# A decoder stack on one core: stream attention outputs normalised with head rows on the partitions, closing products in column tiles

## The chip, the cores and the metric

The kernel runs on one core of one Trainium2 chip. The metric is the device time of one execution in microseconds; the time of a kernel is the median over its runs.

## The reference, cut to what matters

Two decoder layers on a sequence of 2048 rows of 256 features, with a context of 1601 rows. What the change touches is the self-attention and the cross-attention of the second layer (16 heads of 16 features each), whose outputs are projected, added to the input and normalised:

```python
qkv = (jnp.einsum('bnd,ed->bne', x, qkv_w) + qkv_b).reshape(b, n, H, 3 * HD)
q, k, v = ...
attn = jax.nn.softmax(jnp.einsum('bhqd,bhkd->bhqk', q, k) * SCALE, axis=-1)
out = jnp.einsum('bhqk,bhkd->bhqd', attn, v)
...
x = _layernorm(x + _L1_attn_ref(x, ...))         # out @ fc_w.T + fc_b + x
x = _layernorm(x + _L1_xattn_ref(ctx_1024, ctx_1024, x, ...))   # out @ Wo + bo
```

Before it run the first layer (banded attention with a GELU network, causal cross-attention, a network with eight low-rank experts), behind it the eight-expert network of the second layer.

## The kernel before

The second layer's two attentions run as one stream, `decoder_attention`. `Plan` writes its order out by hand. A **step** is one segment (0 self-attention, 1 cross-attention), one chunk of 512 queries (`QC`, four per segment) and one group of four heads (`GH`): 2 x 4 x 4 = 32 steps. A **pair** is a step and one tile of 128 keys: 16 pairs in a step of segment 0, 13 in one of segment 1, 464 in all. `plan.first[s]` is the first pair of step s. Every engine walks over the pairs p = 0 ... 495 in order, and at each p does what the plan lists there.

In a pair TensorE (PE) does the scores of four heads (L1481, bf16, four column tiles of 32 columns side by side), the products with the values of the pair before (L1499, f32, again 32 columns per head, so that the four heads fill `ps_o`), and, between them, the products for the row maxima of the **next** step (L1291), which go through a ring of three PSUM banks `ps_m` (`plan.bank`, `bank_free`). ScalarE (ACT) takes the exponentials (L1612). VectorE (DVE) reduces each maxima product (L1304): 64 of them in a step of segment 0, 64 in one of segment 1, of which 16 have 128 columns only. The same ring carries all small products of the stream.

SyncE (SP) issues the transfers in program order. At p = first[s+1] it issues `load(s+3)`, held until the scores up to that pair are done: 12 transfers, six of keys (L1269) and six of queries (L1272), to rows taken six apart.

The end of a step s: ACT copies `ps_o` to `o_raw` (`copy_o`, L1605) at p = first[s+1]. Its row 32j + 16 holds the sum of the exponentials of head j, rows 32j to 32j + 15 the unnormalised output. Two pairs later (`TURN_AT`) PE transposes it in four full-array f32 transposes to a ring bank (`turn_out`, L1509), and DVE takes the reciprocal of 16 columns (L1726) and multiplies into `o_tok` (L1728), both in `normalise`. After four steps a chunk is complete, and at the four pairs that follow PE transposes each token tile back (`turn_tokens`, L1519, two transposes), ACT copies it to `o_fm` (L1622), and a pair later PE does the output product (`out_product`, L1532, two full-array f32 products of 256 columns), which DVE adds to `x_tok` (L1739) and follows with the statistics. Root, scaling and a transpose back (L1542) come later. The projections of segment 1's keys, queries and values are woven in as units (L1558, 16 of them) and value tiles (L1567, 13 of them), full-array f32 products too.

Of the kernel before, what the change touches and what calls it, by code (L numbers as in the profile page):

```python
# [1107 lines left out]
class Plan:  # L1108
# [11 lines left out]
    TURN_AT = 2  # L1120

    def __init__(self, segments):
        self.segments = segments
        self.steps = [(si, c, g) for si in range(len(segments)) for c in range(NQ) for g in range(NG)]
        self.pairs, self.first = [], []
        for s, (si, c, g) in enumerate(self.steps):
            self.first.append(len(self.pairs))
            self.pairs += [(s, i, kt) for i, kt in enumerate(segments[si].at.key_tiles(c))]
        self.total = len(self.pairs)
        self.first.append(self.total)  # L1130
        self.chunks = [(si, c) for si in range(len(segments)) for c in range(NQ)]
        self.out_at = [self.first[s + 1] + (self.TURN_AT if s + 1 < len(self.steps) else 1)
                       for s in range(len(self.steps))]
# [42 lines left out]
    def close_chunks(self, project_next):  # L1176


        for k, (si, c) in enumerate(self.chunks):
            start = self.out_at[NG * k + NG - 1]  # L1180
            for a in range(QT):
                self.tasks[start + 1 + a].append(("turn", k, a))
                self.tasks[start + 2 + a].append(("prod", k, a))
            self.tasks[start + 7].append(("root", k))
            self.tasks[start + 8].append(("inverse", k))
            for a in range(QT):
                self.tasks[start + 8 + a].append(("scale", k, a))
                self.tasks[start + 9 + a].append(("fm", k, a))
            if project_next and si == 0:
                for m in range(DT):  # L1190
                    self.unit(start + 15 + 2 * m, "q", m, c * QC, QC)
                for a in range(QT):
                    self.tasks[start + 20 + a].append(("base", k, a))
# [18 lines left out]
    def set_ring(self, banks):  # L1212

        self.banks, self.order = banks, []
        for p in range(self.total + 32):
            if p < self.total:
                self.order += [("max", x) for place in self.places[p] for x in place]
            self.order += [("out", s) for s in range(len(self.steps)) if self.out_at[s] == p]
            self.order += [task for task in self.tasks[p] if task[0] in ("turn", "prod", "fm", "unit", "v")]
        self.index = {step: r for r, step in enumerate(self.order)}  # L1220
# [115 lines left out]
def decoder_attention(nc, name, plan, maxima, q_st, x_tok, x_fm, ctx_fm, t, cst):  # L1336
# [17 lines left out]
    with ExitStack() as ctx:  # L1354
# [3 lines left out]
        def sem(n):  # L1358
# [3 lines left out]
        inv_den = sb("inv_den", [P, QT, GH, 1], F32)  # L1362
        o_raw = sb("o_raw", [P, QC], F32)
        prob = sb("prob", [P, 2, GH, QC], F32)
        o_tok = sb("o_tok", [P, 2, QT, D], F32)
        o_fm = sb("o_fm", [P, 2, DT, P], F32)
# [16 lines left out]
        s_scores, s_prob, s_pv, s_msc, s_mred, s_ocopy, s_turn, s_inv_den, s_norm = map(  # L1383
            sem, ("scores", "prob", "pv", "msc", "mred", "ocopy", "turn", "inv_den", "norm"))
        s_oturn, s_ofm, s_prod, s_base, s_y, s_stat, s_mv, s_std, s_inv, s_x, s_xturn, s_xfm = map(
            sem, ("oturn", "ofm", "prod", "base", "y", "stat", "mv", "std", "inv", "x", "xturn", "xfm"))
# [8 lines left out]
        def step_of(p):  # L1395
            return plan.pairs[p][0]

        @block.sync
        def _(sp):
# [20 lines left out]

            sp.dma_start(ctx_sb[:, :, 0:CTX], ctx_fm.rearrange("(t p) n -> p t n", p=P)).then_inc(s_ctx, 16)
# [9 lines left out]
            for p in range(plan.total + 32):  # L1431
# [14 lines left out]
        def _(pe):  # L1446
            def bank_free(step):
# [7 lines left out]
                elif kind == "out":  # L1455
                    pe.wait_ge(s_norm, user[1] + 1)
                elif kind == "turn":
                    pe.wait_ge(s_ofm, user[1] * QT + user[2] + 1)
# [44 lines left out]
            def turn_out(s):  # L1503

                step = ("out", s)
                pe.wait_ge(s_ocopy, s + 1)
                bank_free(step)
                for a in range(QT):
                    mm = pe.transpose(plan.bank(step)[:, a * P:(a + 1) * P], o_raw[:, a * P:(a + 1) * P],  # L1509
                                      cst["ident"][:, :])  # L1510
                mm.then_inc(s_turn, 1)

            def turn_tokens(step):

                k, a = step[1:]
                pe.wait_ge(s_norm, NG * (k + 1))
                bank_free(step)
                for m in range(DT):
                    mm = pe.transpose(plan.bank(step)[:, m * P:(m + 1) * P], o_tok[:, k % 2, a, m * P:(m + 1) * P],  # L1519
                                      cst["ident"][:, :])  # L1520
                mm.then_inc(s_oturn, 1)

            def out_product(step):
# [22 lines left out]
            def unit_product(step):  # L1546
# [10 lines left out]
                for d in range(DT):  # L1557
                    mm = pe.matmul(plan.bank(step)[:, 0:n], w_sb[:, 0 if side == "q" else 1, d, m * P:(m + 1) * P],  # L1558
                                   src[:, d, k:k + n], start=(d == 0), stop=(d == DT - 1))
                mm.then_inc(s_mm, 1)  # L1560

            def v_product(step):
# [3 lines left out]
                for d in range(DT):  # L1566
                    mm = pe.matmul(plan.bank(step)[:, 0:D], ctx_sb[:, d, i * P:(i + 1) * P], w_sb[:, 2, d, :],  # L1567
                                   start=(d == 0), stop=(d == DT - 1))
                mm.then_inc(s_vmm, 1)

            for p in range(plan.total + 32):
# [11 lines left out]
                for s in range(len(plan.steps)):  # L1583
                    if plan.out_at[s] == p:
                        turn_out(s)
                for task in plan.tasks[p]:
                    if task[0] == "turn":
                        turn_tokens(task)
                    elif task[0] == "prod":
# [9 lines left out]
        def _(act):  # L1599
            def copy_o(s):  # L1600

                act.wait_ge(s_pv, plan.first[s + 1])
                if s > 0:
                    act.wait_ge(s_turn, s)
# [9 lines left out]

            def copy_tokens(step):

                k, a = step[1:]
                n = k * QT + a
                act.wait_ge(s_oturn, n + 1)
                if n >= 2:  # L1620
                    act.wait_ge(s_prod, n - 1)
                act.activation(o_fm[:, n % 2, :, :], plan.bank(step)[:, 0:D].rearrange("p (a b) -> p a b", a=DT),  # L1622
                               ACT.Copy).then_inc(s_ofm, 1)
# [30 lines left out]
            for p in range(plan.total + 32):  # L1654
# [5 lines left out]
                for task in plan.tasks[p]:  # L1660
                    if task[0] == "turn":
                        copy_tokens(task)
                    elif task[0] == "root":
# [42 lines left out]
        def _(dve):  # L1706
# [9 lines left out]
            def normalise(s):  # L1716

                si, c, g = plan.steps[s]
                k = s // NG
                heads = plan.bank(("out", s))[:, :].rearrange("p (a j d) -> p a j d", a=QT, j=GH)  # L1720
                dve.wait_ge(s_turn, s + 1)
                if s > 0:
                    dve.wait_ge(s_norm, s)
                if g == 0 and k >= 2:
                    dve.wait_ge(s_oturn, QT * (k - 1))
                dve.reciprocal(inv_den[:, :, :, :], heads[:, :, :, SH:SH + 1]).then_inc(s_inv_den, 1)  # L1726
                dve.wait_ge(s_inv_den, s + 1)
                dve.tensor_tensor(o_tok[:, k % 2, :, g * GH * SH:(g + 1) * GH * SH]  # L1728
                                  .rearrange("p a (j d) -> p a j d", d=SH), heads[:, :, :, 0:SH],
                                  inv_den[:, :, :, :].to_broadcast((P, QT, GH, SH)), ALU.mult).then_inc(s_norm, 1)  # L1730
# [49 lines left out]
            for p in range(plan.total + 32):  # L1780
# [3 lines left out]
                for s in range(len(plan.steps)):  # L1784
                    if plan.out_at[s] == p:
                        normalise(s)
# [754 lines left out]
def decoder_kernel(nc, t, out):  # L2541

    nc.disable_value_cache = True
    with ExitStack() as ctx:
# [9 lines left out]
        y_slots = nc.dram_tensor("y_slots", (EXPERT_TILES * P, D), F32).ap()  # L2554
        s_zero = nc.alloc_semaphore("slots_cleared")
# [59 lines left out]
        with ExitStack() as c:  # L2615
# [11 lines left out]
            decoder_attention(nc, "d1", plan, maxima, q_st, x_tok, x_fm, t["ctx_fm"], t, cst)  # L2627
# [87 lines left out]
```

## Time and profile before

| | |
|---|---|
| median of 3 runs (lowest to highest) | 3201.78 us (3201.13 to 3211.98) |
| profiled execution, its own time | 3196.11 us |
| its span | 3194.4 us |
| mean granted TensorE clock | 0.938 of full speed |
| busy, whole span | PE 2806.6 us (88%), DVE 2064.1 (65%), ACT 1568.5 (49%), POOL 224.4 (7%) |
| the stream: first scores, last copy of `ps_o` | 1321.9 us, 2718.8 us |

The busy shares are of the whole program; the stream is some 1400 us of it. Of the windows in the first group below, one is a plain step of segment 0, the other a plain step of segment 1. Times below are from the span's start. A matmul's record overlaps the next one's, so the price of a group on PE is read from the start of one group to the start of the next, and not from its length. PE groups of x4 are four column tiles side by side.

### The profile page before, as it was taken

The page shows a single profiled execution, that of the slowest core. Times are in us where ns is not written, and L with a number is a line of the kernel's source. Part 1 is how long each engine was busy: PE and PEld are TensorE (multiplying, and loading weights), DVE is VectorE, ACT ScalarE, POOL GpSimd, SP SyncE. Part 2 cuts the span into 40 slices and gives each one's busy share as a digit, 9 for nine tenths or more (in the row PEclk, how much of TensorE's full clock was granted, in tenths as well). Part 3 has the DMA queues.
Part 4 walks back from the last instruction along what each step waited for, and adds up shares of the span by engine and source line. Part 5 has one row for each costly group of instructions (what it writes and reads, how often), then busy time and mean ns, then how long its engine had stood idle before and what let it go on. Part 6 is the DMA issues. An engine that isn't in the chain of part 4 may idle for free. (4 is left out here: it accounts for less than half of the span.)

```text
span 3194.4 us, 83729 instructions
## 1 busy us (share of the span) xinstructions
PE 2806.6 (88%) x34974; PEld 1416.8 (44%) x34975; DVE 2064.1 (65%) x4240; ACT 1568.5 (49%) x2122; POOL 224.4 (7%) x295
## 2 busy tenths in 40 slices
PE   6677987999996997799999999999999999369993
PEld 3465552444534564134434343443433333246662
DVE  4335136888855235688999898988998995312224
ACT  2223222666672322266767776776666768123331
POOL 2001201000001002300000000000000000210003
PEclk9888997999997999699999999999999999589997
DMA  5322023011001003312112112111111110611102
GB/s 155 102 60 67 27 72 100 13 39 39 3 2 37 1 0 109 99 42 67 34 53 51 53 36 60 44 44 51 42 49 44 44 44 2 249 49 33 33 31 89
DMA packets 112871, 173.46 MB, mean 54 GB/s; under 512 B 17882, under 2 KB 88427, under 8 KB 112147
## 3 DMA queue, kind: packets, MB, share of 16 engines
q1 hardware_dynamic: 109460, 160.11, 17.5%
q0 software_dynamic: 3072, 8.39, 0.8%
q8 instruction: 266, 4.36, 0.6%
q14 instruction: 73, 0.60, 0.1%
HBM read 127.63 MB, written 40.51 MB: 53 GB/s over the span
## 5 line engine op out<-in xcount | busy, mean ns | idle before, releaser
L1304 DVE TENSOR_REDUCE d_part_max<-d_ps_m 128x1 f32<-128x512 f32 (+1 forms) x1964 | 1128.1, 631 | 89.0 <-PE d_ps_m L1291 52.7
L1612 ACT ACTIVATE d_prob<-d_ps_s 128x1024 f32<-128x1024 f32 x928 | 898.7, 1022 | 345.7 <-PE d_ps_s L1481 338.9
L1291 PE MATMUL d_ps_m<-k_st,q_st 97*32 97x512 bf16 (+1 forms) x5296 | 479.2, 361 | 20.5 <-DVE d_part_max L1304 16.9
L1481 PE MATMUL d_ps_s<-q_st,k_st 98*32 98x512 bf16 x5104 | 439.5, 382 | 9.7 <-ACT d_prob L1612 8.4
L690 DVE TENSOR_REDUCE x_part_max<-x_att_ps_m 128x1 f32<-128x512 f32 (+2 forms) x578 | 309.6, 587 | 50.2 <-PE x_att_ps_m L675 22.7
L936 ACT ACTIVATE x_att_prob<-x_att_ps_s 128x1024 f32<-128x1024 f32 (+3 forms) x296 | 258.8, 920 | 138.8 <-PE x_att_ps_s L817 82.8
L1499 PE MATMUL d_ps_o<-d_prob,a_values 128*32 128x512 f32 x2048 | 265.0, 592 | 0.0
L1291 PEld LDWEIGHTS d_ps_m<-k_st,q_st 97*32 97x32 bf16 x5296 | 141.5, 95 | 274.2 <-DVE d_part_max L1304 127.8
L1291 PE MATMUL d_ps_m<-q_st 97*32 97x512 bf16 (+1 forms) x2560 | 230.9, 361 | 2.2 <-DVE d_part_max L1304 0.4
L1481 PEld LDWEIGHTS d_ps_s<-q_st,k_st 98*32 98x32 bf16 x5104 | 136.6, 97 | 196.0 <-issue 82.4
L1499 PE MATMUL d_ps_o<-d_prob,x_values 128*32 128x512 f32 x1664 | 215.5, 593 | 0.4 <-ACT d_prob L1612 0.4
L666 PE MATMUL x_att_ps_m<-k_st,q_st 97*32 97x512 bf16 (+3 forms) x2312 | 202.8, 343 | 3.3 <-DVE x_part_max L690 2.7
L1481 PE MATMUL d_ps_s<-q_st 98*32 98x512 bf16 x2320 | 200.2, 380 | 2.6 <-ACT d_prob L1612 2.6
L817 PE MATMUL x_att_ps_s<-q_st,k_st 98*32 98x512 bf16 (+3 forms) x2368 | 192.3, 358 | 11.0 <-DMA q_st<-x_neg_row 6.5
L2465 ACT ACTIVATE l1f_h_cols<-l1f_ps_t,l_b 128x128 f32<-128x128 f32 x312 | 84.9, 383 | 141.1 <-PE l1f_ps_t L2423 141.1
L2431 PE MATMUL l1f_ps_y<-l_w,l1f_h_cols 128*128 x624 | 144.4, 384 | 2.2 <-ACT l1f_h_cols L2465 2.2
L2412 PE MATMUL l1f_ps_h<-l_w,l1f_x_cols 128*128 x312 | 142.2, 599 | 1.3 <-ACT l1f_x_cols L2456 0.7
L850 PE MATMUL x_att_ps_o<-x_att_prob,v_grp 128*32 128x512 f32 (+3 forms) x1184 | 139.4, 542 | 0.4 <-ACT x_att_prob L936 0.4
L2510 DVE COPY l1f_h_rows<-l1f_ps_h 128x512 f32<-128x512 f32 x78 | 54.0, 692 | 126.0 <-PE l1f_ps_h L2412 126.0
L2431 PEld LDWEIGHTS l1f_ps_y<-l_w,l1f_h_cols 128*128 128x128 f32 x624 | 115.4, 190 | 20.9 <-issue 4.0
L1291 PEld LDWEIGHTS d_ps_m<-q_st 97*32 97x32 bf16 x2560 | 68.1, 95 | 123.8 <-DVE d_part_max L1304 53.4
L690 DVE TENSOR_REDUCE a_part_max<-a_att_ps_m 128x1 f32<-128x256 f32 (+1 forms) x102 | 41.5, 415 | 100.5 <-PE a_att_ps_m L675 93.9
(326 smaller groups left out, 3344.8 us busy)
## 6 DMA issues: line engine op xcount, KB each, us to landing
k_st<-parts_k SPq DMA_DIRECT2D x90, 256.0 KB, 5.5
k_st<-parts_k SPq DMA_DIRECT2D x90, 208.0 KB, 4.4
l_w<-in_l_w SPq DMA_DIRECT2D x16, 1024.0 KB, 14.1
q_st<-parts_q SPq DMA_DIRECT2D x48, 256.0 KB, 4.7
q_st<-parts_q SPq DMA_DIRECT2D x192, 64.0 KB
q_st<-parts_k SPq DMA_DIRECT2D x30, 256.0 KB
q_st<-parts_k SPq DMA_DIRECT2D x30, 208.0 KB
parts_q<-a_proj_parts SPq DMA_DIRECT2D x16, 384.0 KB, 2.5
```

The source lines that it names most:

```text
L666: mm = pe.matmul(out[q:q + COLUMNS, :], q_st[0:rows, slot, j, start:start + COLUMNS], k_st[0:rows, slot, j, k:k + w], start=(half == 0), s ...
L690: dve.tensor_reduce(self.part[:, h * QT + a, i:i + 1], bank[:, 0:w], AX.X, ALU.max).then_inc(s_read, 1)
L817: mm = pe.matmul(bank[q:q + COLUMNS, hh, q0:QC], k_st[0:ROW_MAX + 1, bass.ds(slot(g), 1), h, key:key + COLUMNS], q_st[0:ROW_MAX + 1, bass. ...
L850: mm = pe.matmul(ps_o[32 * j:32 * j + 32, q0:QC], v_grp[:, kt, j, :], prob[:, k % 2, j, q0:QC], start=(i == 0), stop=(i == n - 1), skip_gr ...
L936: act.activation(prob[:, k % 2, 2 * u:2 * u + 2, q0:QC], bank[:, :, q0:QC], ACT.Exp, scale=scale).then_inc(s_prob, 1)
L1291: mm = pe.matmul(bank[q:q + COLUMNS, 0:w], self.query(s, h, ROW_MASK + 1, a * P + q, COLUMNS), self.key(s, h, ROW_MASK + 1, k, w), start=T ...
L1304: dve.tensor_reduce(self.part[:, h * QT + a, i:i + 1], bank[:, 0:w], AX.X, ALU.max).then_inc(s_read, 1)
L1481: mm = pe.matmul(ps_s[u][k:k + COLUMNS, hh, :], maxima.key(s, h, ROW_MAX + 1, kt * P + k, COLUMNS), maxima.query(s, h, ROW_MAX + 1, 0, QC) ...
L1499: mm = pe.matmul(ps_o[32 * j:32 * j + 32, :], value_block(segments[si].values, kt, g * GH + j), prob[:, p % 2, j, :], start=(i == 0), stop ...
L1612: act.activation(prob[:, p % 2, 2 * u:2 * u + 2, :], ps_s[u][:, :, :], ACT.Exp, scale=scale).then_inc(s_prob, 1)
L2412: mm = pe.matmul(ps_h[hh][:, :], x_cols[:, m, :], w1_sb[:, bass.ds(e, 1), m, hh * QC:(hh + 1) * QC], start=(m == 0), stop=(m == DT - 1))
L2431: mm = pe.matmul(ps_y[:, 0:D], h_cols[:, f, :], w2_sb[:, bass.ds(e, 1), f, :], start=(f == 0), stop=(f == FT - 1))
```

## The change

`turn_out`, `turn_tokens`, `copy_tokens` and `normalise` go. In their place, with `half` for two steps (128 head rows, one of the two feature tiles of a chunk; 16 halves):

- `gather(s)` on SP, at p = first[s+1], **behind `load(s+3)` in the same queue**: for each of the four heads one transfer of the row of sums (2 KB, to `sums` as 16 partitions x 32) and one of the 16 output rows (32 KB, to their place in `o_fm`, features on the partitions). 8 transfers a step. For the last half the sums go straight to `den`, repeated over 16 partitions.
- `invert(half)` on DVE, 2 pairs into the step after the half (`GATHERED_AT`): waits for all 16 transfers of the half, and takes the reciprocal of 128x32 in place.
- `spread(half)` on SP, at 4 pairs (`SPREAD_AT`): writes the 128x32 to DRAM, waits for its landing, and issues 8 transfers that read it back repeated, to `den` 128x512.
- `divide(half)` on DVE, at 7 pairs (`DIVIDED_AT`): `o_fm` times `den`, 128x512. The output products of a chunk start one pair after.
- The output products, the units and the value tiles are each split into four column tiles of 32.

```diff
@@ Plan
-    TURN_AT = 2
+    GATHERED_AT = 2
+    SPREAD_AT = 4
+    DIVIDED_AT = 7
...
         for k, (si, c) in enumerate(self.chunks):
-            start = self.out_at[NG * k + NG - 1]
+            start = self.divided_at[DT * k + DT - 1]
             for a in range(QT):
-                self.tasks[start + 1 + a].append(("turn", k, a))
-                self.tasks[start + 2 + a].append(("prod", k, a))
-            self.tasks[start + 7].append(("root", k))
+                self.tasks[start + 1 + a].append(("prod", k, a))
+            self.tasks[start + 6].append(("root", k))
...
@@ sync
+            def gather(s):
+                half = half_of(s)
+                k, m = half // DT, half % DT
+                sp.wait_ge(s_ocopy, s + 1)
+                if half >= 1:
+                    sp.wait_ge(s_kept if half < plan.halves - 1 else s_norm,
+                               16 * half if half < plan.halves - 1 else half)
+                if k >= 2:
+                    sp.wait_ge(s_prod, QT * (k - 1))
+                for j in range(GH):
+                    first = (s % (NG // DT) * GH + j) * SH
+                    rows = slice(first, first + SH)
+                    row = o_raw[32 * j + SH:32 * j + SH + 1, :]
+                    if half < plan.halves - 1:
+                        sp.dma_start(sums[rows, :], row.rearrange("p (r n) -> p r n", r=SH)).then_inc(s_gather, 16)
+                    else:
+                        sp.dma_start(den[rows, :], row.rearrange("p (o n) -> p o n", o=1)
+                                     .to_broadcast((1, SH, QC))).then_inc(s_gather, 16)
+                    sp.dma_start(o_fm[rows, k % 2, m, :], o_raw[32 * j:32 * j + SH, :]).then_inc(s_gather, 16)
+
+            def spread(half):
+                sp.wait_ge(s_inv_den, half + 1)
+                sp.dma_start(inverses[half].rearrange("(p n) -> p n", p=P), sums[:, :]).then_inc(s_kept, 16)
+                sp.wait_ge(s_kept, 16 * (half + 1))
+                if half >= 1:
+                    sp.wait_ge(s_norm, half)
+                for j in range(P // SH):
+                    sp.dma_start(den[j * SH:(j + 1) * SH, :], inverses[half:half + 1, j * QC:(j + 1) * QC]
+                                 .to_broadcast((SH, QC))).then_inc(s_spread, 16)
...
                 for s in range(2, len(plan.steps)):
                     if plan.first[s - 2] == p:
                         load(s)
+                for s in range(len(plan.steps)):
+                    if plan.first[s + 1] == p:
+                        gather(s)
+                for half in range(plan.halves - 1):
+                    if plan.spread_at[half] == p:
+                        spread(half)
...
@@ tensor (turn_out and turn_tokens removed)
-                pe.wait_ge(s_ofm, n + 1)
+                pe.wait_ge(s_norm, DT * (k + 1))
                 bank_free(step)
                 for m in range(DT):
-                    mm = pe.matmul(plan.bank(step)[:, 0:D], o_fm[:, n % 2, m, :],
-                                   wo_sb[:, plan.chunks[k][0], m, :], start=(m == 0), stop=(m == DT - 1))
+                    for q in range(0, P, COLUMNS):
+                        start = a * P + q
+                        mm = pe.matmul(plan.bank(step)[q:q + COLUMNS, 0:D],
+                                       o_fm[:, k % 2, m, start:start + COLUMNS],
+                                       wo_sb[:, plan.chunks[k][0], m, :], start=(m == 0), stop=(m == DT - 1),
+                                       skip_group_check=True)
... (unit_product and v_product are split in the same way)
@@ scalar (copy_tokens removed)
                 if s > 0:
-                    act.wait_ge(s_turn, s)
+                    act.wait_ge(s_gather, 16 * 2 * GH * s)
@@ vector (normalise removed)
+            def invert(half):
+                dve.wait_ge(s_gather, 16 * 2 * GH * (NG // DT) * (half + 1))
+                some = sums if half < plan.halves - 1 else den
+                dve.reciprocal(some[:, :], some[:, :]).then_inc(s_inv_den, 1)
+
+            def divide(half):
+                k, m = half // DT, half % DT
+                if half < plan.halves - 1:
+                    dve.wait_ge(s_spread, 16 * (P // SH) * (half + 1))
+                dve.wait_ge(s_inv_den, half + 1)
+                dve.tensor_tensor(o_fm[:, k % 2, m, :], o_fm[:, k % 2, m, :], den[:, :], ALU.mult).then_inc(s_norm, 1)
...
                     for place in plan.places[p]:
                         reductions(place)
-                for s in range(len(plan.steps)):
-                    if plan.out_at[s] == p:
-                        normalise(s)
+                for half in range(plan.halves):
+                    if plan.gathered_at[half] == p:
+                        invert(half)
+                for half in range(plan.halves):
+                    if plan.divided_at[half] == p:
+                        divide(half)
```

## Rows read from the trace of the kernel before

**Rows 1.** Windows: length, busy PE, PEld, DVE, ACT, POOL, PE clock, DMA share, GB/s.

```profile
1688.89:1731.63 42.74, 42.64 (x653) 18.04 (x649) 40.69 (x69) 31.51 (x34) 0.00 (x0) 1.00 0.21 48
...
2230.58:2267.23 36.65, 36.16 (x581) 14.48 (x577) 34.15 (x68) 25.80 (x28) 0.00 (x0) 1.00 0.16 49
```

**Rows 2.** Timeline, end of step 3: start, length, engine, line, groups merged (x).

```profile
1544.63 0.60 ACT L1605 ACTIVATE d_o_raw<-d_ps_o 128x512 f32<-128x512 f32 x1
...
1548.38 0.60 SPq L1272 DMA_DIRECT2D q_st<-parts_q  x1
...
1549.51 0.43 PE L1291 MATMUL d_ps_m<-q_st 97*32 97x512 bf16 x4
...
1550.46 0.40 PE L1481 MATMUL d_ps_s<-q_st,k_st 98*32 98x512 bf16 x4
...
1550.60 0.25 DVE L1726 RECIPROCAL d_inv_den<-d_ps_m 128x16 f32<-128x16 f32 x1
```

**Rows 3.** Timeline at the end of step 27: SP's last load, DVE's reciprocal.

```profile
2582.71 0.59 SPq L1272 DMA_DIRECT2D q_st<-parts_q  x1
...
2584.86 0.25 DVE L1726 RECIPROCAL d_inv_den<-d_ps_m 128x16 f32<-128x16 f32 x1
```

**Rows 4.** Timeline of PE in pairs of chunk 0's closing.

```profile
1552.00 1.03 PE L1499 MATMUL d_ps_o<-d_prob,a_values 128*32 128x512 f32 x8
...
1552.86 0.39 PE L1291 MATMUL d_ps_m<-q_st 97*32 97x512 bf16 x4
...
1553.54 0.40 PE L1481 MATMUL d_ps_s<-q_st,k_st 98*32 98x512 bf16 x4
...
1555.94 0.39 PE L1291 MATMUL d_ps_m<-q_st 97*32 97x512 bf16 x4
...
1557.54 0.40 PE L1481 MATMUL d_ps_s<-q_st,k_st 98*32 98x512 bf16 x4
...
1567.92 0.39 PE L1291 MATMUL d_ps_m<-q_st 97*32 97x512 bf16 x4
...
1569.30 0.40 PE L1481 MATMUL d_ps_s<-q_st,k_st 98*32 98x512 bf16 x4
...
1574.30 0.39 PE L1291 MATMUL d_ps_m<-q_st 97*32 97x512 bf16 x4
...
1574.52 0.39 PE L1481 MATMUL d_ps_s<-q_st,k_st 98*32 98x512 bf16 x4
```

**Rows 5.** Transfers by line: issue ns min/median/max; time to landing.

```profile
L291 SPq DMA_DIRECT2D k_st<-key_masks x16: 237/257/376, 21.8 to 457.7; - x16
...
L1269 SPq DMA_DIRECT2D k_st<-parts_k x132: 587/597/2205, 1237.6 to 2626.4; - x132
...
L1315 SPq DMA_DIRECT2D q_st<-d_neg_row x32: 552/579/612, 1309.6 to 2683.2; - x32
...
DMA to landing us min/median/max: 1.7/1.7/3.4
```

**Rows 6.** Windows around an idle stretch of PE in another stage, same columns.

```profile
1183.50:1187.60 4.10, 0.08 (x1) 0.00 (x0) 2.75 (x8) 1.26 (x3) 0.00 (x0) 1.00 0.00 0
1187.60:1199.00 11.40, 11.39 (x48) 9.73 (x49) 3.97 (x11) 1.15 (x3) 0.00 (x0) 0.85 0.00 1
...
1249.00:1260.00 11.00, 8.94 (x52) 2.77 (x52) 7.91 (x13) 2.53 (x4) 1.62 (x2) 0.84 0.04 13
```

**Rows 7.** DVE's groups in the stream: total busy us, mean ns, idle before.

```profile
L1728 DVE TENSOR_TENSOR d_o_tok<-d_ps_m,d_inv_den 128x256 f32<-128x256 f32 x32 | 13.6, 425 | 1.1
...
L1761 DVE TENSOR_TENSOR d_rest<-d_exact,d_parts 128x512 f32<-128x512 f32 x12 | 8.3, 692 | 29.3 <-ACT d_parts L1650 20.3 <-ACT d_exact L1647 9.1
...
L1747 DVE RECIPROCAL d_inv<-d_std 128x4 f32<-128x4 f32 x8 | 1.4, 173 | 0.5 <-ACT d_std L1627 0.4
```

**Rows 8.** The stream's end: last copy of `ps_o`, last output product.

```profile
2718.79 0.60 ACT L1605 ACTIVATE d_o_raw<-d_ps_o 128x512 f32<-128x512 f32 x1 [1.19 <-PE d_ps_o L1499]
...
2730.73 1.57 PE L1532 MATMUL d_ps_m<-d_wo,d_o_fm 128*128 128x256 f32 x4 [0.47 <-ACT d_o_fm L1622]
```

More of the change, by code:

```diff
@@ L1131, in __init__ @@
         self.chunks = [(si, c) for si in range(len(segments)) for c in range(NQ)]
-        self.out_at = [self.first[s + 1] + (self.TURN_AT if s + 1 < len(self.steps) else 1)
-                       for s in range(len(self.steps))]
+        self.halves = len(self.steps) // (NG // DT)
+        self.gathered_at, self.spread_at, self.divided_at = (
+            [self.first[(i + 1) * (NG // DT)] + (later if i + 1 < self.halves else 0) for i in range(self.halves)]
+            for later in (self.GATHERED_AT, self.SPREAD_AT, self.DIVIDED_AT))
         self.place_entries()
@@ L1217, in set_ring @@
                 self.order += [("max", x) for place in self.places[p] for x in place]
-            self.order += [("out", s) for s in range(len(self.steps)) if self.out_at[s] == p]
-            self.order += [task for task in self.tasks[p] if task[0] in ("turn", "prod", "fm", "unit", "v")]
+            self.order += [task for task in self.tasks[p] if task[0] in ("prod", "fm", "unit", "v")]
         self.index = {step: r for r, step in enumerate(self.order)}
@@ L1382, in decoder_attention @@
         ps_o = ctx.enter_context(nc.psum_tensor(f"{name}_ps_o", [P, QC], F32))
[L1383 to L1386, printed above, removed]
+        s_scores, s_prob, s_pv, s_msc, s_mred, s_ocopy, s_gather, s_inv_den, s_kept, s_spread, s_norm = map(
+            sem, ("scores", "prob", "pv", "msc", "mred", "ocopy", "gather", "inv_den", "kept", "spread", "norm"))
+        s_prod, s_base, s_y, s_stat, s_mv, s_std, s_inv, s_x, s_xturn, s_xfm = map(
+            sem, ("prod", "base", "y", "stat", "mv", "std", "inv", "x", "xturn", "xfm"))
         s_w, s_ctx, s_wo, s_pad, s_ones, s_mm, s_exact, s_high, s_rest, s_mid, s_low, s_vmm, s_vout = map(
@@ L1501, in times_v @@
                 mm.then_inc(s_pv, 1)
[L1503 to L1521, printed above, removed]
             def out_product(step):
@@ L1557, in unit_product @@
                 for d in range(DT):
-                    mm = pe.matmul(plan.bank(step)[:, 0:n], w_sb[:, 0 if side == "q" else 1, d, m * P:(m + 1) * P],
-                                   src[:, d, k:k + n], start=(d == 0), stop=(d == DT - 1))
+                    for q in range(0, P, COLUMNS):
+                        start = m * P + q
+                        mm = pe.matmul(plan.bank(step)[q:q + COLUMNS, 0:n],
+                                       w_sb[:, 0 if side == "q" else 1, d, start:start + COLUMNS],
+                                       src[:, d, k:k + n], start=(d == 0), stop=(d == DT - 1), skip_group_check=True)
                 mm.then_inc(s_mm, 1)
@@ L1566, in v_product @@
                 for d in range(DT):
-                    mm = pe.matmul(plan.bank(step)[:, 0:D], ctx_sb[:, d, i * P:(i + 1) * P], w_sb[:, 2, d, :],
-                                   start=(d == 0), stop=(d == DT - 1))
+                    for q in range(0, P, COLUMNS):
+                        start = i * P + q
+                        mm = pe.matmul(plan.bank(step)[q:q + COLUMNS, 0:D], ctx_sb[:, d, start:start + COLUMNS],
+                                       w_sb[:, 2, d, :], start=(d == 0), stop=(d == DT - 1), skip_group_check=True)
                 mm.then_inc(s_vmm, 1)
@@ L1582, in _ @@
                     maxima_products(plan.places[p][3])
-                for s in range(len(plan.steps)):
-                    if plan.out_at[s] == p:
-                        turn_out(s)
                 for task in plan.tasks[p]:
-                    if task[0] == "turn":
-                        turn_tokens(task)
-                    elif task[0] == "prod":
+                    if task[0] == "prod":
                         out_product(task)
@@ L1613, in exponentials @@
                                    scale=scale).then_inc(s_prob, 1)
[L1615 to L1623, printed above, removed]
             def root(k):
@@ L1660, in _ @@
                 for task in plan.tasks[p]:
-                    if task[0] == "turn":
-                        copy_tokens(task)
-                    elif task[0] == "root":
+                    if task[0] == "root":
                         root(task[1])
@@ L1714, in reductions @@
                     maxima.reduce(dve, x, plan.bank(("max", x)), s_mred, count)
[L1716 to L1730, printed above, removed]
+            def invert(half):
[8 more added lines that the diff above has]
+                dve.tensor_tensor(o_fm[:, k % 2, m, :], o_fm[:, k % 2, m, :], den[:, :], ALU.mult).then_inc(s_norm, 1)
             def add_product(step):
@@ L2626, in decoder_kernel @@
                     StepAhead(nc, "a1_proj", plan, maxima, q_st, cst), cst, values[0][:, :])
[L2627 removed]
+            decoder_attention(nc, "d1", plan, maxima, q_st, x_tok, x_fm, t["ctx_fm"],
+                              inverses, t, cst)
         shared.close()
```

27 lines of the change are left out of this document (12 added, 15 removed).

## The prediction, made blind

> **What bounds the kernel now.** I read the slices of the page first: between 1400 and 2718 us, the stream, PE is at nine tenths in all slices and its clock at full. Next the windows by step. In a plain step of segment 0 PE is busy 42.64 of 42.74 us and DVE 40.69; in one of segment 1 PE 36.16 and DVE 34.15 of 36.65 [rows 1]. Both engines are nearly full, PE first, and they are tied to each other by a ring of three banks: a gain on PE is passed on, and so is any stop of DVE longer than three maxima products. Last the timeline at the ends of steps, with SP beside the engines. There the reader is to see two distances. A group that stays in column tiles takes 0.22 us to the next (1574.30 to 1574.52 [rows 4]); whatever runs on the full array takes more than its own passes. And SP, idle for most of a step, is at its busiest just where the change puts its transfers: in step 3 the last of the 12 loads is issued until 1548.98, while ACT copied `ps_o` at 1544.63 and DVE reaches its place two pairs on at 1550.60 [rows 2].
>
> **What goes away on PE.** `turn_out`: from the maxima product ahead of it to the next scores 0.95 us [rows 2] against 0.22 without, so 0.73 a step; 31 steps outside the tail: 22.6 us. `turn_tokens`: alone 1553.54 - 1552.86 = 0.68, less 0.22, 0.46; beside an output product 1557.54 - 1555.94 = 1.60 against 1.38 for the product alone (1567.92 to 1569.30), so 0.22 [rows 4]. A chunk has one alone and three beside: 1.12; seven chunks: 7.8 us.
>
> **Column tiles.** An output product costs 1.38 - 0.22 = 1.16 us on the full array. In column tiles it has the same f32 passes, two times 256 columns, as the values' product has with 512: 1552.00 to 1552.86, 0.86 us, weights included [rows 4]. So 0.30 less for each of 28 products: 8.4 us. The 16 units and 13 value tiles enter and leave the full array in the same way; I give each the same 0.30: 8.7 us. Bounds: nothing (should four small weight loads for one not hide), and 0.30 for all 57. The row of the values' product, where they do hide, is nearest, so I take all of it.
>
> The Trainium skill speaks on both sides here. TensorEngine Tiling (Array Packing), Key Properties, says that a change of tiling mode drains the engine, which is what the 0.30 would be. Restrictions and Gotchas says that column tiles exclude the fast weight load. By the second rule the tiled products would be longer than I count; the trace's 0.86 us for a full set of tiled f32 products shows no such cost.
>
> **DVE.** Removed are 0.25 [rows 2] and 0.43 [rows 7] a step, 1.36 a half. Added are the reciprocal of 128x32 and a 128x512 multiply, 0.69 [rows 7]. Reciprocals: 0.17 for 4 columns [rows 7], 0.25 for 16 [rows 2], so 6 ns a column and 0.35 for 32; at the least 0.17. DVE gains 0.3 a half. That is far less than PE gains, and in segment 1 the two already wait for each other: 0.49 us of its plain step are lost to PE [rows 1]. There a step can gain between 0.16 (DVE's share) and 0.73; I take the middle and give back 0.285 x 15 = 4.3 us. ACT's copies (`copy_tokens`) are hidden: ACT is busy 31.5 of 42.7 us [rows 1].
>
> Gain: 22.6 + 7.8 + 8.4 + 8.7 - 4.3 = 43.2 us; bounds 26 (no gain from tiles) and 48.
>
> **The new wait.** `invert` stands in DVE's queue at the place where `normalise` stood, and needs all eight transfers of the step that just ended. SP holds them behind `load(s+3)` in program order. In step 3 the load's issues end 1.62 us before DVE arrives, in step 27 at 2583.30, 1.56 us before [rows 2, 3]; the odd steps between them lie around these, with 1.6 as the mean of the 13 (0.5 to 2.6). An issue takes SP 0.60 for a load, 0.58 for the row of maxima, both with 16 partitions on a side, 0.26 for one partition to one [rows 5], and 0.04 between two. I take 0.58 in all, near the upper end where the like rows are. The last of eight starts 7 x 0.58 = 4.1 us after the load, and lands 1.7 us later [rows 5]. DVE waits 4.1 + 1.7 - 1.6 = 4.2 us. Bounds: spacing 0.30 gives 2.2, spacing 0.64 gives 4.6.
>
> The Trainium skill, DMA: Bandwidth & Descriptors, Anatomy of one DMA, puts the fixed cost of a transfer at about 2.0 us; the trace has 1.7 for one inside SBUF. By the page the wait would be 0.3 us longer.
>
> Behind the waiting reciprocal are all reductions. PE may run three maxima products ahead, then stops in front of the fourth with scores, value products and exponentials behind it. DVE is at most one product behind when it stops, so PE would go on for 1.5 us (1552.1 if I walk through the pair after 1550.46 without `turn_out`); it starts again one reciprocal and one reduction after the landing, at 1550.6 + 4.2 + 0.35 + 0.69 (a reduction of 512 columns, like the multiply) = 1555.8. Idle 3.7 us, and some tenths more from an emptied ring: the stall is about DVE's own wait, 4.2 us. A step has no slack to take it back, since PE is the full engine. Steps 1, 3, ... 27 have loads: 14 x 4.2 = 58.8 us; step 29 has none, 0.3 us. Even steps have no `invert`.
>
> **The clock.** In the stream it is granted in full [rows 1]. Elsewhere an idle stretch of 4 us, 1183.5 to 1187.6, is followed by 11.4 us at a mean of 0.85, and the 11.0 us from 1249, behind another idle stretch, are at 0.84 [rows 6]. At two levels, 2.4 and 1.2 GHz, that is 11.4 x 0.15 / 0.5 = 3.4 us at the lower one, or 1.7 us of work lost. With 3.7 us idle per half I take this each time: 14 x 1.7 = 23.8 us. Bounds: nothing, and twice that.
>
> **Spread and divide.** After `inv_den` SP issues the write, which lands 1.7 later, then eight reads, the last 4.1 later, landing 1.7: 1.7 + 4.1 + 1.7 = 7.5 us. DVE is at `divide` five pairs on, 5 x 42.7 / 16 = 13 us. So no wait, with 5.4 us to spare. The next maxima's row is sent eight or more pairs later; `load(s+3)` is ahead of it all. Nothing of value queues behind SP's waits.
>
> **The tail.** The last copy ends at 2719.4, and the last product at 2732.3 [rows 8]. After: the last of eight transfers starts at 2723.5 and lands at 2725.2; a reciprocal of 512 columns, at 6 ns each, 3.2 us; multiply 0.69: 2729.1. Four products of 0.86, or 1.7 at half speed: 2732.5 to 2735.9. I take +2 us (0 to 4).
>
> **Sum.** -43.2 + 58.8 + 0.3 + 23.8 + 2 = +41.7 us on the execution's own 3196.1, which is its span plus 1.7: 3237.8. The median of the runs is 5.7 above it, so 3243.5 as a median.
>
> **The rivals.** *Short waits, no change.* If SP issues at about 0.40, the wait is 7 x 0.40 + 1.7 - 1.6 = 2.9 us, 41 us in all; PE idles 2.4, and the clock may hold. -43.2 + 41 + 2 = 0: 3202. The 0.26 of a one-partition transfer speaks for it, the 0.58 and 0.60 of 16 partitions against.
>
> *Faster: the transfers are nearly covered.* The place is the same, DVE at `invert`. With a spacing of 0.30 it waits 2.2 us, 31 us in all, with no drop of the clock and the full 48 of gain: -48 + 31 + 0 = -17, 3185 as a median; each further 0.5 us less of wait takes off 7. It decides at a wait of (48 - 16) / 14 = 2.3 us. What speaks for it is that the eight transfers are small, and that I gave the stall no slack at all; against it, that the landing alone, 1.7, is more than the 1.6 us at hand.
>
> *Slower: the spread is late too.* If the write to DRAM and the reads from it, repeated over 16 partitions, come 7 us later in all than the 1.7 of SBUF makes them, `divide` waits 2 us as well, 15 times: 3243.5 + 30 = 3273. It decides from the 5.4 us that are to spare. That a round over DRAM stands in no row speaks for it; that the loads are done by then, against.
>
> **How the numbers follow.** The forecast's own case 0.53, spread late 0.09, short waits 0.17, covered 0.21. This kernel's measurement can tell about 0.5%, 16 us, from no change. In the forecast's case a small part falls short of +16, when wait and clock come out low together. Slower 0.60, same 0.18, faster 0.22. The own case reaches from -48 + 50 + 14 = +16 to -26 + 64 + 36 + 4 = +78: 3218 to 3280. The range takes in the short waits and the nearer part of the covered case, and leaves out under 0.2: 3180 to 3283.
>
> **What would show it.** In the profile after: DVE's idle time ahead of the reciprocal of 128x32, released by a transfer, 14 times 3.5 to 5 us; the same on PE ahead of L1291 and of ACT; stretches of half clock after each; SP's issues of `gather` directly behind the load's. Plain even steps should fall from 42.7 to some 42.0. The output product with its tiles should take 0.86 us to the next group. The prediction is wrong if the transfers are issued faster than 0.4 us apart, if the wait is taken up by something that I called full, or if a tiled f32 product costs over 1.2 us.

## The result, and the profile after

The changed kernel takes 3290.68 us in the median (3289.53 to 3291.99, 4 runs) against 3201.45 before: a ratio of 1.0271, 95% interval 1.0256 to 1.0286. It is slower by 2.7%, some 89 us. The forecast was 3243.5, slower by 42, with a range up to 3283: the side was right, the size less than half of what came.

From the page after: busy time by engine, the slices of PE, DVE and the clock.

```profile
PE 2802.6 (85%) x35514; PEld 1425.0 (43%) x35515; DVE 2063.1 (63%) x4208; ACT 1557.4 (47%) x2090; POOL 223.8 (7%) x295
...
PE   6586978999987987799999999988998999459992
...
DVE  4335138888843237688888888877887886412224
...
PEclk9788987999998997899999999999999999679996
```

No engine is busy for longer: PE 4 us less than before, DVE and ACT 1 and 11 less. The program is 94 us longer all the same, so PE stands idle for more of it. That is not the whole loss, for PE's busy time hides some: matmuls at half clock take longer (below). Where the idleness is, the waits after between 1380 and 2810 us tell (engine and line, who was waited for: us in all, times, longest us):

```profile
ACT d_prob L1635 <- PE d_ps_s L1520: 447.1, 430, 9.5
PEld d_ps_m L1293 <- DVE d_part_max L1306: 288.2, 539, 7.1
...
DVE d_sums L1731 <- DMA d_o_fm<-d_o_raw: 79.6, 15, 6.8
PE d_ps_m L1293 <- DVE d_part_max L1306: 78.8, 40, 6.6
```

The third row is the new one: 15 times DVE stands in front of the reciprocal of a half's sums until the last gathering transfer has landed, 5.3 us in the mean. The first, second and fourth stood in the kernel before too, but smaller (ACT waited 316 us for the scores there, and the two rows of the ring were 160 and 3.3 us); what they have grown by is the same stops handed on, to PE by the ring and from PE to ACT.

One stop, at the end of step 5, in the timeline after:

```profile
1658.38 0.60 SPq L1274 DMA_DIRECT2D q_st<-parts_q  x1
...
1659.07 0.59 SPq L1441 DMA_DIRECT2D d_sums<-d_o_raw  x1
...
1662.23 1.17 SPq L1445 DMA_DIRECT2D d_o_fm<-d_o_raw  x1
...
1664.07 0.59 SPq L1445 DMA_DIRECT2D d_o_fm<-d_o_raw  x1
1666.04 0.35 DVE L1731 RECIPROCAL d_sums<-d_sums 128x32 f32<-128x32 f32 x1 [5.33 <-DMA d_o_fm<-d_o_raw]
...
1666.99 0.40 PE L1293 MATMUL d_ps_m<-k_st,q_st 97*32 97x512 bf16 x4 [4.62 <-DVE d_part_max L1306]
```

Read from the top: the load's last issue ends at 1658.98; the eight gathering transfers follow it, 0.63 us from start to start, but one of them is held for 1.17; the last starts at 1664.07 and has landed 2.0 us later. DVE had arrived at 1660.71. PE stood still for 4.62 us. The load ends as far ahead of DVE's arrival as before [rows 2, 3], 1.7 us, but now that is the start of the eight transfers.

Three windows after: the 10 us around the next stop (it begins at 1753.1), then the stop above, and the 4 us behind it.

```profile
1754.00:1764.00 10.00, 5.61 (x56) 1.97 (x60) 4.92 (x9) 2.05 (x2) 0.00 (x0) 0.66 0.14 35
...
1662.37:1666.99 4.62, 0.00 (x0) 0.00 (x1) 0.95 (x3) 0.24 (x1) 0.00 (x0) 1.00 0.08 17
1666.99:1671.00 4.01, 4.01 (x40) 1.30 (x44) 3.63 (x6) 2.05 (x2) 0.00 (x0) 0.57 0.23 45
```

After such a stop PE works on at the lower of its two levels, 1.2 GHz: a mean of 0.57 over 4.01 us is 3.4 us of it; 0.66 over ten is 6.8 us. In the whole stream PE is at 1.2 GHz for 102 us, in 17 stretches, where it was never so before.

The whole stream, first to last copy of `ps_o`, by window before, after, and in the first experiment below:

```profile
1393.44:2718.79 1325.35, 1297.50 (x18798) 528.71 (x18794) 1167.29 (x2177) 938.84 (x1032) 20.83 (x30) 1.00 0.16 45
```

```profile
1395.67:2809.86 1414.19, 1302.99 (x19242) 537.98 (x19234) 1161.56 (x2145) 929.49 (x1003) 20.79 (x30) 0.96 0.18 48
```

```profile
1396.65:2700.95 1304.30, 1264.68 (x19242) 546.54 (x19234) 1156.21 (x2145) 928.43 (x1003) 20.34 (x30) 1.00 0.20 52
```

The stream is 88.8 us longer: PE is idle for 83.4 us more of it (111.2 against 27.9) and busy for 5.5 more. Against e1_late, which has the same work and its clock nearly full, PE is idle for 71.6 us more and busy for 38.3 more; the latter I read as the half clock, since nothing else about the work differs. The stages ahead of the stream took 2.2 us more in this execution, and what follows it 3.1 more, but both lie within the scatter: over the nine profiled executions of this document the first copy comes between 1393.4 and 1403.2 us, and what follows the last one takes 472.8 to 482.0.

### The profile page after: what moved, and what is told of

The parts are those of the page before. It is cut to its first block and busy times, and to the rows that moved or that the text cites. A ratio compares the mean times of both kernels' runs of the same rounds, so it can differ in the third digit from the quotient of the medians.

```text
span 3288.6 us, 85064 instructions
## 1 busy us (share of the span) xinstructions
PE 2802.6 (85%) x35514; PEld 1425.0 (43%) x35515; DVE 2063.1 (63%) x4208; ACT 1557.4 (47%) x2090; POOL 223.8 (7%) x295
## 5 line engine op out<-in xcount | busy, mean ns | idle before, releaser
L1293 PE MATMUL d_ps_m<-k_st,q_st 97*32 97x512 bf16 (+1 forms) x5296 | 499.6, 370 | 73.0 <-DVE d_part_max L1306 64.8
L1520 PE MATMUL d_ps_s<-q_st,k_st 98*32 98x512 bf16 x5104 | 455.0, 389 | 9.9 <-ACT d_prob L1635 8.5
L936 ACT ACTIVATE x_att_prob<-x_att_ps_s 128x1024 f32<-128x1024 f32 (+3 forms) x296 | 258.8, 921 | 140.0 <-PE x_att_ps_s L817 83.4
L1293 PEld LDWEIGHTS d_ps_m<-k_st,q_st 97*32 97x32 bf16 x5296 | 151.3, 97 | 350.6 <-DVE d_part_max L1306 206.4
L1538 PE MATMUL d_ps_o<-d_prob,a_values 128*32 128x512 f32 x2048 | 272.0, 601 | 0.0
L1293 PE MATMUL d_ps_m<-q_st 97*32 97x512 bf16 (+1 forms) x2560 | 240.2, 370 | 30.9 <-DVE d_part_max L1306 28.9
L1520 PEld LDWEIGHTS d_ps_s<-q_st,k_st 98*32 98x32 bf16 x5104 | 147.5, 99 | 182.9 <-issue 77.0
L1538 PE MATMUL d_ps_o<-d_prob,x_values 128*32 128x512 f32 x1664 | 225.4, 618 | 0.4 <-ACT d_prob L1635 0.4
L1520 PE MATMUL d_ps_s<-q_st 98*32 98x512 bf16 x2320 | 206.9, 388 | 5.1 <-ACT d_prob L1635 5.1
```

The source lines that it names most:

```text
L936: act.activation(prob[:, k % 2, 2 * u:2 * u + 2, q0:QC], bank[:, :, q0:QC], ACT.Exp, scale=scale).then_inc(s_prob, 1)
L1293: mm = pe.matmul(bank[q:q + COLUMNS, 0:w], self.query(s, h, ROW_MASK + 1, a * P + q, COLUMNS), self.key(s, h, ROW_MASK + 1, k, w), start=T ...
L1520: mm = pe.matmul(ps_s[u][k:k + COLUMNS, hh, :], maxima.key(s, h, ROW_MAX + 1, kt * P + k, COLUMNS), maxima.query(s, h, ROW_MAX + 1, 0, QC) ...
L1538: mm = pe.matmul(ps_o[32 * j:32 * j + 32, :], value_block(segments[si].values, kt, g * GH + j), prob[:, p % 2, j, :], start=(i == 0), stop ...
```

## Experiments

All ratios are to the kernel before, on the same chip.

**Move the three places back (e1_late).**

```diff
-    GATHERED_AT = 2
-    SPREAD_AT = 4
-    DIVIDED_AT = 7
+    GATHERED_AT = 5
+    SPREAD_AT = 7
+    DIVIDED_AT = 10
```

> The changed kernel with the reciprocal at 5 pairs into the step, the spread at 7, the multiply at 10 (in place of 2, 4, 7); nothing else. Theory (the cost is DVE's wait for transfers that stand behind the load in SP's queue, 79.6 us, and the half clock that follows each of the stops, some 50 us): both go, because DVE arrives 13 us after the copy instead of 6; clock 1.0 through the stream; 3201 - 43 + 2, about 3160. Rival 1 (the transfers or their traffic slow the stream wherever they are waited for): at least 3201. Rival 2 (the half clock comes from the tiled closings, not from idleness): waits gone, clock still low in places, about 3210.

Measured: 3182.13 us, ratio 0.9923 (0.9907 to 0.9940). Ahead of the last step no wait of DVE for a transfer is left, and the clock over the stream is 1.00 (last row above). So the same transfers, waited for later, leave the kernel faster than before, and rival 1 falls; rival 2 falls with the clock, since the tiled closings are all there. The whole loss sits in the two or three pairs between the copy and the reciprocal. But the gain is short: on this chip the kernel before took 3207.77, so 25.6 us were gained where 41 were expected, and the stream is 1304.3 us, 21.0 below before, where I had 43.2. That half of the error is taken up in e4, e6 and e7.

The 1.00 is rounded. With the places moved, the root of a chunk of segment 0 comes at the start of a step, right behind `copy_o`, and its two table loads hold ACT's exponentials back. PE stands still for 1.91 us, at most 1.4 before, and once in this kernel the clock drops behind it:

```profile
1591.34 1.28 ACT L1640 ACT_TABLE_LOAD   x1
...
1592.95 1.28 ACT L1635 ACT_TABLE_LOAD   x1
...
1595.32 0.40 PE L1520 MATMUL d_ps_s<-q_st 98*32 98x512 bf16 x4 [1.91 <-ACT d_prob L1635]
```

```profile
1595.32:1602.59 7.27, 7.24 (x79) 2.41 (x82) 4.71 (x8) 4.80 (x6) 0.00 (x0) 0.77 0.40 79
```

**One pair later (e2_gathered3).** The places are 3, 5 and 8.

> The changed kernel with the reciprocal at 3 pairs into the step, the spread at 5, the multiply at 8. Theory: DVE's wait shrinks by one pair, 2.6 to 2.8 us, to 2.6 us, 14 times, 37 us; PE then idles 2 us a half. If so short an idleness leaves the clock alone: 3201 - 43 + 37 + 2 = 3197. If each is still followed by 3.4 to 6.8 us at half clock: 3221 to 3245. Rival (the wait is not one for a fixed landing time): the wait stays near 5 us and the time near 3290.

Measured: 3243.25 us, ratio 1.0119 (1.0098 to 1.0139).

```profile
  DMA d_o_fm<-d_o_raw: 44.3, 13
```

One pair, 2.6 to 2.8 us, takes 2.1 us off each of these 13 waits: 3.4 in the mean, 5.5 for the same halves before (the first half and the one of step 29 wait no more). It behaves as a wait for a landing at a fixed time, and the rival falls. The time is that of the half-clock branch. Four windows of this kernel show two stops, one with the half clock behind it and one without: an idle stretch of 2.92 us and the 9.4 us after it, one of 2.45 and the 10.9 after it.

```profile
1653.71:1656.63 2.92, 0.00 (x0) 0.00 (x0) 0.95 (x3) 0.24 (x1) 0.00 (x0) 1.00 0.09 21
1656.63:1666.00 9.37, 9.37 (x120) 3.42 (x124) 7.97 (x13) 4.99 (x6) 0.00 (x0) 0.82 0.16 32
1848.62:1851.07 2.45, 0.00 (x1) 0.00 (x0) 0.95 (x3) 0.26 (x1) 0.00 (x0) 1.00 0.07 14
1851.07:1862.00 10.93, 10.93 (x168) 4.33 (x172) 10.81 (x18) 7.56 (x8) 0.00 (x0) 1.00 0.10 27
```

**The gathering transfers ahead of the load (e3_gather_first).**

```diff
-                for s in range(2, len(plan.steps)):
-                    if plan.first[s - 2] == p:
-                        load(s)
                 for s in range(len(plan.steps)):
                     if plan.first[s + 1] == p:
                         gather(s)
+                for s in range(2, len(plan.steps)):
+                    if plan.first[s - 2] == p:
+                        load(s)
```

> The changed kernel with the 8 gathering transfers ahead of the load of the same pair in SP's queue, pairs 2, 4, 7 as in the change. Theory (it is the place in the queue): last gathering transfer issued 0.6 + 7 x 0.63 after the copy's start plus 0.6, landing 2.0 later, 7.1 us after the copy's start, against DVE's arrival at 6.0: wait 1.1 us, 14 times, 15 us; no half clock; 3201 - 43 + 15 + 2 = 3176. The load is 9 us later and still in time. Rival (eight small transfers are slow by themselves): wait stays above 4 us, time above 3250. Rival (the later load is missed): PE waits for its keys ahead of the next maxima.

Measured: 3263.5 us, ratio 1.0164 (1.0135 to 1.0194), and 3176 was expected. The waits of DVE:

```profile
  DMA d_o_fm<-d_o_raw: 19.5, 15
...
  DMA d_den<-inverse_sums: 33.0, 14
```

The first wait did what it should, 1.3 us each. A second one took its place: the load now stands between the gathering transfers and the spread. In DVE's timeline the reciprocal is at 1659.54, and the multiply waits:

```profile
1659.54 0.36 DVE L1731 RECIPROCAL d_sums<-d_sums 128x32 f32<-128x32 f32 x1 [0.94 <-DMA d_o_fm<-d_o_raw]
...
1675.74 0.69 DVE L1739 TENSOR_TENSOR d_o_fm<-d_o_fm,d_den 128x512 f32<-128x512 f32 x1 [3.39 <-DMA d_den<-inverse_sums]
```

while SP issues the write of the inverses only at 1667.01, 7 us after it could:

```profile
1667.01 0.58 SPq L1450 DMA_DIRECT2D inverse_sums<-d_sums  x1
```

I had asked who waits for the later load and not what stands behind it in the queue. It was my third rival, a late spread, brought about by the experiment itself. It supports the theory of the queue: with the same engine issuing, the first wait went from 5.3 to 1.3 us by the order alone. That there would be no half clock wasn't tested, as the new waits brought their own.

**Column tiles alone, on the kernel before (e4_tiles_only).** The edit of the diff in `out_product`, `unit_product` and `v_product`, the rest as before.

> The kernel before with the output products, the units and the value tiles in four column tiles, and nothing else of the change. Theory: each of 57 gives 0.30 us, no leaving of the tiled mode: 3201 - 17 = 3184. Rival (four weight loads in place of one, without the fast load): no gain or a loss, 3201 or more.

Measured: 3200.11 us, ratio 0.9977 (0.9968 to 0.9987), 7.5 us where 17 were expected. On PE the tiled product has the length I gave it, 0.86 us from its start to the next group's:

```profile
1569.23 1.04 PE L1533 MATMUL d_ps_m<-d_wo,d_o_fm 128*32 128x256 f32 x16
1570.09 0.39 PE L1481 MATMUL d_ps_s<-q_st,k_st 98*32 98x512 bf16 x4
```

So the weight loads hide, as the values' product had shown. Where a transpose follows, as behind three of a chunk's four products while `turn_tokens` is there, the full array is entered in any case:

```profile
1557.16 0.39 PE L1291 MATMUL d_ps_m<-q_st 97*32 97x512 bf16 x4
1557.38 1.04 PE L1533 MATMUL d_ps_m<-d_wo,d_o_fm 128*32 128x256 f32 x16
1558.35 0.44 PE L1519 MATMUL d_ps_m<-ident,d_o_tok 128*128 128x128 f32 x2
1558.71 0.40 PE L1481 MATMUL d_ps_s<-q_st,k_st 98*32 98x512 bf16 x4
```

1.55 us against 1.60 before [rows 4]. This accounts for 21 products outside the tail at 0.25 each, 5.3 of the 9.6 us missing. The rest isn't explained by it: from the second to the third copy of `ps_o`, 16 pairs that hold seven units and value tiles and no `turn_tokens`, the length fell from 52.71 to 51.89 us, 0.8 where seven times 0.30 were expected.

**GpSimd issues the gathering transfers (e5_pool_gather).**

```diff
-                        sp.dma_start(sums[rows, :], ...).then_inc(s_gather, 16)
+                        pool.dma_start(sums[rows, :], ...).then_inc(s_gather, 16)
 ... (all of gather(s), called in GpSimd's walk over the pairs)
```

> The changed kernel with the eight gathering transfers of a step issued by GpSimd, which is idle there, in place of SP; pairs 2, 4, 7 as in the change. Theory (the stream's time is its 1304 us without waits, plus DVE's waits, plus half of the time at half clock; the wait is the place in SP's queue behind the load): the transfers start 5 us earlier. If GpSimd needs 0.6 us for each, the last lands 6.8 us after the copy's start against DVE's 6.0: wait 0.8 us, 12 us in all, clock full, 3195 against 3202 before. If it needs 1 us for each: wait 3.6 us, half clock behind it, about 3250. Rival (a transfer of 16 partitions inside SBUF is slow whoever issues it): wait above 4 us in either case.

Measured: 3205.83 us, ratio 1.0013 (1.0003 to 1.0024). DVE waits 25.7 us in 14 times, 1.8 each, neither of the two figures I gave: GpSimd issues faster than I had assumed, and its transfers land later.

```profile
L1692 POOL DMA_DIRECT2D d_o_fm<-d_o_raw x128: 484/484/534, 1404.8 to 2742.8; - x128
...
DMA to landing us min/median/max: 1.7/3.1/4.7
```

Same places, same eight transfers, another queue: 5.3 us of wait become 1.8, though each transfer lands 1.1 us later than from SP. With e3, where SP kept them, this leaves the place behind the load as the cause; the rival falls.

**The full array again, with late places (e6_late_full).** e1_late with the three products as before.

> As e1_late (5, 7, 10), but output products, units and value tiles on the full array again: what is left is only the transposes, the transfers and the division. My own price of the tiles is 17 us, which would put it 17 above e1_late, at 3199 or a ratio of 0.9977. By the run with the tiles alone (-7.5) it is 8 above, 0.9947. If the tiles gain more once no transposes stand beside the products, nearer to the first.

Measured: 3186.14 us, ratio 0.9947 (0.9931 to 0.9964), the second figure, though the interval is 10 us wide and the digit is luck. The stream is 1313.4 us. So transposes out, transfers and division in give 11.9 us (I had 26.1: 22.6 + 7.8 - 4.3), and the tiles 9.1 more.

**GpSimd does the multiply (e7_late_pool).**

```diff
+                for half in range(plan.halves - 1):
+                    if plan.divided_at[half] == p:
+                        k, m = half // DT, half % DT
+                        pool.wait_ge(s_spread, 16 * (P // SH) * (half + 1))
+                        pool.tensor_tensor(o_fm[:, k % 2, m, :], o_fm[:, k % 2, m, :], den[:, :],
+                                           ALU.mult).then_inc(s_norm, 1)
... (on DVE, `divide` is left for the last half alone)
```

> As e1_late, but the multiply of 128x512 is done by GpSimd in all halves but the last. e1_late's plain steps are 42.1 us without, and 42.7 with the reciprocal and the multiply on DVE (36.0 and 36.6 in segment 1). Theory (the gain on PE is eaten in those steps by DVE's new work, 1.04 us a half): the steps with a multiply fall to about 42.2, 15 x 0.5 = 8 us below e1_late, ratio 0.990. Rival (they are slower because the closing of a chunk or the transfers stand in them): no change from e1_late, 0.9923.

Measured: 3171.83 us, ratio 0.9903 (0.9886 to 0.9919), 6 us below e1_late by the ratios (8 were expected), which were taken on two chips and have intervals that overlap; the streams say it better, 1298.8 against 1304.3 us, 5.5 less. It beats both kernels. The steps by window in e1_late show what is repaired: a plain step with the division, and one without.

```profile
1862.47:1905.14 42.67, 42.54 (x653) 21.06 (x649) 40.71 (x68) 32.12 (x35) 0.00 (x0) 1.00 0.22 52
1905.14:1947.22 42.08, 41.42 (x630) 23.53 (x626) 39.69 (x68) 30.22 (x32) 0.00 (x0) 1.00 0.24 58
```

Before, both took 42.74 [rows 1]. The step without gains 0.66, near PE's 0.73; the one with gives nearly all of it back: DVE, which has got 1.04 us of new work in it, is busy 40.71 of 42.67. In e7_late_pool the first of the two falls to 42.10 (1869.21 - 1827.11 between its copies).

That accounts for the plain steps, and leaves most of the missing gain. It lies in the steps in which a chunk is closed. The two steps of one closing (chunk 1) before, and the same two in e1_late:

```profile
1731.63:1783.89 52.26, 50.69 (x685) 21.50 (x681) 46.91 (x86) 37.45 (x46) 0.00 (x0) 1.00 0.16 41
1783.89:1833.12 49.23, 48.06 (x661) 18.18 (x656) 43.12 (x73) 33.82 (x39) 4.45 (x6) 1.00 0.20 58
```

```profile
1729.62:1776.30 46.68, 46.02 (x713) 23.93 (x707) 44.30 (x81) 31.50 (x35) 0.00 (x0) 1.00 0.22 53
1776.30:1828.77 52.47, 49.32 (x689) 18.61 (x684) 44.46 (x76) 38.20 (x45) 4.43 (x6) 1.00 0.22 57
```

101.49 us became 99.15: 2.3 gained, where my prices for what they hold (two `turn_out`, the four `turn_tokens`, four products, two units) come to 4.4. PE's busy time fell by 3.4, and its idle time rose from 2.7 to 3.8. Over the stream, the 15 steps of closings gained 12.0 us of some 30 that the prices give them, the 16 others 9.1 of some 16.

**All of them together.** The stream's length as 1304.3 us (e1_late), plus DVE's waits for transfers; what is left over stands beside two measures of the clock, half of the time that the trace shows at 1.2 GHz, and PE's busy time above e1_late's 1264.7, for the same work:

| | stream | waits | left over | half of the time at 1.2 GHz | PE busy above e1_late |
|---|---|---|---|---|---|
| changed kernel | 1414.2 | 79.6 | 30.3 | 51.2 | 38.3 |
| e3_gather_first | 1380.7 | 52.5 | 23.9 | 30.7 | 32.9 |
| e2_gathered3 | 1360.9 | 44.3 | 12.3 | 18.8 | 19.7 |
| e5_pool_gather | 1335.4 | 25.7 | 5.4 | 10.2 | 13.2 |
| e1_late | 1304.3 | 0 | 0 | 1.7 | 0 |

The order of the left-over follows the clock. It is below both measures. For the second the trace has a reason: PE idles for less than DVE waits, 4.62 us in the stop shown, where DVE waited 5.33, so the waits are counted too high as a loss of PE, 79.6 for 71.6 of added idle time. No kernel was run with the stops and without the half clock, so the split between them rests on the busy times.

## Why the prediction was wrong in size

The sum had -43.2 (gain), +58.8 and +0.3 (wait), +23.8 (clock), +2 (tail): +41.7. Measured on the profiled executions: -21.0, +79.6, +30.3, +3.1, and 2.2 ahead of the stream: +94.2.

- **What bounds the kernel**: right for PE in the plain steps, and too light on DVE. I took its 2 us of idle time in a step of segment 0 as room.
- **The gain, first failed term.** -21.0 in place of -43.2 (of which 1.5 were for units and value tiles ahead of the first copy, outside this window). The single prices on PE held where they were read: 0.66 of 0.73 in a step without division, 0.86 for a tiled product. What failed is the adding up, the step "a gain on PE is passed on". PE's busy time fell by 32.8 us (1297.5 to 1264.7), where the prices come to some 46, and its idle time rose by 11.8 (27.9 to 39.6), where 4.3 were given back. Three parts of this were measured. After "That is far less than PE gains" I charged DVE's new work in segment 1 alone; it costs the step it stands in some 0.6 us in both segments, 15 times, and moving the multiply away gave back 5.5 us (e7). The tiles are worth 9.1 (e6 against e1) in place of 17.1. And most of what is missing lies in the closings of the chunks, where products, transposes, additions and the root meet, and for which I had added up prices read one at a time. What each of these costs there wasn't separated, and the cause stays open; DVE's total work alone isn't it, for in e7, where DVE is busy 20 us less than in the kernel before, the stream is only 26.6 us shorter than before, and not some 46. The Trainium skill's rule against the tiles (TensorEngine Tiling (Array Packing), Restrictions and Gotchas, the fast weight load) isn't why: the 0.86 us leaves no room for it.
- **The wait, second failed term.** The place, its cause and its count were right; its size was 5.5 us in place of 4.2 in the 14 steps with a load, and step 29 waited 2.0 in place of 0.3 (together the 5.3 above). The row values I took were at fault: issues come 0.63 apart (I chose 0.58 over the 0.64 of the loads, my own upper end), in 20 of the 32 steps one of the eight is held, to between 0.9 and 1.7 us, and a landing takes 2.0 (median of 128) where the row of maxima, landing in an idle queue, took 1.7. Here the Trainium skill did better than the row: DMA: Bandwidth & Descriptors, Anatomy of one DMA, has some 2.0 us of fixed cost, and this trace agrees, though the section speaks of transfers that GpSimd issues, and those took 3.1 in e5_pool_gather.
- **The clock**: 23.8 forecast, 30.3 measured as what is left over, 38.3 by PE's busy time. Right in kind and too low, as most stops were followed by 6.8 us at the lower level and not 3.4. It was charged because a row of another stage showed it [rows 6]; e2 shows that shorter stops bring less of it, though not by their length alone. My upper end, twice 23.8, covered it.
- **Spread and divide**: no wait in the changed kernel, as said. e3 shows how little it takes to make one.
- **The tail**: +3.1 against +2, within the scatter of what follows. By its own rows, from the last copy of `ps_o` to the first transpose of `x_tok`, it took 15.70 us before and 19.25 after, 3.55 more, inside my 0 to 4. The reciprocal of 512 columns took 3.35 us and the one of 32 took 0.353, as worked out (3.2, 0.35).

Both failed terms erred to the same side, the clock with them, and each alone (22 and 21 us) would have left the time inside the range. That the side came out right is no luck, since the wait and the clock behind it are what e1_late removes. The range was built from the bounds of single terms, but its upper end left out that gain and wait could miss together.

## What to carry to other kernels

A transfer that is moved into a queue starts when what stands ahead of it has been issued, and each issue on SP with 16 partitions on a side cost 0.6 us here, for 2 KB as for 256 KB; ask for every new wait what is ahead of it in the queue, and for every reordering what is now behind. When two engines are both over nine tenths busy, work taken from one is worth only what the other leaves: here 1.04 us of new work on the second cost its step 0.6, in both segments. Prices read in plain stretches don't add up where many small tasks meet; read such a stretch by itself, from start to end. And a stop of the busiest engine costs more than its length, if the clock is let down behind it: three pairs later, the same change was a gain of 0.8%.

## What the runs showed of the hardware

- PE's clock in the stream: in e2_gathered3 an idle stretch of 2.45 us passed at full clock, and one of 2.92 was followed by 3.4 us at 1.2 GHz; yet one of 2.32 (2385.49 to 2387.81) was followed by 7.19 us at a mean of 0.76, 3.5 us of half clock, and in e1_late one of 1.91 (1593.41 to 1595.32) by 7.27 us at a mean of 0.77, 3.3 us of half clock, so the length alone doesn't decide. In the changed kernel one of 5.3 (1753.1 to 1758.4) was followed by 6.8 us.
- Eight transfers of 2 and 32 KB inside SBUF, over 16 partitions, cost SP the same 0.59 us to issue (median of 120 and of 128). GpSimd issues them in 0.48, and those of 32 KB land in 3.1 us in place of 2.0.
- VectorE's reciprocal costs 6.25 ns a column: 353 ns for 32, 3353 ns for 512.
